# Cross-attention with residual and LayerNorm: residual sum kept in PSUM, output bias by matmul, queries projected one batch a step

## What is computed

```python
Q = (query @ Wq.T + bq).reshape(B, Sq, N_HEADS, D_K).transpose(0, 2, 1, 3)
K = (key_value @ Wk.T + bk)...
V = (key_value @ Wv.T + bv)...
scores = jnp.einsum('bhqd,bhkd->bhqk', Q, K) / np.sqrt(D_K)
attn = jax.nn.softmax(scores, axis=-1)
context = jnp.einsum('bhqk,bhkd->bhqd', attn, V)...
output = context @ W_o.T + b_o
x = output + query
mu = jnp.mean(x, axis=-1, keepdims=True)
var = jnp.mean(jnp.square(x - mu), axis=-1, keepdims=True)
return (x - mu) / jnp.sqrt(var + LN_EPS) * ln_gamma + ln_beta
```

## Time and profile before

| what | value |
|---|---|
| median of 3 runs | 232.86 us (232.59 to 237.04) |
| profiled execution, span from first to last instruction | 230.5 us |
| TensorE matmul busy | 206.8 us (90%) |
| GpSimd busy | 182.9 us (79%) |
| VectorE busy | 181.4 us (79%) |
| ScalarE busy | 172.3 us (75%) |
| mean granted TensorE clock | 0.989 of full speed |

### The profile page before, as it was taken

The page is one execution under the profiler, slowest core; times in us unless marked ns, Lnnn a source line. Parts: engine busy times, 40 slices in busy tenths (PEclk is TensorE's granted clock), DMA queues, the critical chain, the costliest instruction groups (busy, mean ns, idle before and its releaser), DMA issues.

```text
span 230.5 us, 6883 instructions
## 1 busy us (share of the span) xinstructions
PE 206.8 (90%) x2740; PEld 190.9 (83%) x2740; DVE 181.4 (79%) x378; ACT 172.3 (75%) x313; POOL 182.9 (79%) x163
## 2 busy tenths in 40 slices
PE   0999998899999899989999899989998999997930
PEld 0998797799899789978999699969996899997820
DVE  5699977378778977887888878787878787986494
ACT  4589489678778769795888588958796788887440
POOL 9999454877379958997699769975999499999873
PEclk9999999999999999999999999999999999999995
DMA  6946322345611153115321532143124111121022
GB/s 206 331 73 201 62 53 72 117 124 175 159 50 48 46 148 92 50 51 137 92 57 48 129 66 80 60 119 81 46 68 86 43 48 46 57 87 46 3 94 91
DMA packets 24808, 20.96 MB, mean 91 GB/s; under 512 B 10554, under 2 KB 21953, under 8 KB 24776
## 3 DMA queue, kind: packets, MB, share of 16 engines
q1 hardware_dynamic: 23544, 19.26, 30.1%
q10 hardware_dynamic: 1232, 1.26, 1.8%
HBM read 11.32 MB, written 4.19 MB: 67 GB/s over the span
## 4 chain that ended last, share of the span: by engine, by line
PE 52%; POOL 15%; DVE 12%; issue 10%; ACT 7%; DMA 2%; POOLq 0%; DVEq 0%; ACTq 0%
PE ps_s L348 18%; PE ps_x L348 14%; PE ps_acc L348 13%; POOL p_l L1042 9%; PE ps_d L348 6%; DVE result L905 4%; DVE xT_l L764 4%; ACT p_h L684 3%; POOL result L1050 2%; POOL x_rows L1059 2%; DMA w_raw<-in_wkT 2%; POOL rs_y L1071 2%; PE ps_x L509 1%; ACT ctx_h L691 1%; DVE vrest L796 1%
## 5 line engine op out<-in xcount | busy, mean ns | idle before, releaser
L1042 POOL TENSOR_TENSOR p_l<-p,p_h 128x512 f16<-128x512 f32 x80 | 99.1, 1243 | 34.5 <-ACT p_h L684 34.1
L850 DVE TENSOR_REDUCE maxima<-ps_d 128x4 f32<-128x308 f32 x128 | 58.8, 464 | 23.6 <-PE ps_d L348 23.2
L683 ACT ACTIVATE p<-ps_s 128x512 f32<-128x512 f32 x80 | 47.3, 592 | 21.7 <-PE ps_s L348 21.0
L348 PE MATMUL ps_acc<-vblk,p_h 128*128 128x34 bf16 (+1 forms) x960 | 52.0, 183 | 2.0 <-POOL p_l L1042 2.0
L348 PE MATMUL ps_s<-q_low,kblk 128*128 128x256 f32 x192 | 51.2, 298 | 1.1 <-issue 1.0
L348 PEld LDWEIGHTS ps_acc<-vblk,p_h 128*128 128x128 f16 x960 | 43.2, 96 | 10.3 <-issue 3.2
L348 PE MATMUL ps_acc<-vblk,p_l 128*128 128x34 bf16 (+1 forms) x640 | 48.4, 181 | 0.0
L684 ACT ACTIVATE p_h<-ps_s 128x512 f16<-128x512 f32 x80 | 47.2, 590 | 0.0
L348 PE MATMUL ps_s<-q_lo,kblk 128*128 128x256 f32 x160 | 45.0, 282 | 0.0
L348 PE MATMUL ps_d<-kblk,q_low 128*128 128x308 f32 x128 | 41.4, 327 | 0.2 <-DVE maxima L850 0.2
L348 PEld LDWEIGHTS ps_acc<-vblk,p_l 128*128 128x128 f16 x640 | 38.7, 96 | 0.0
(11 more groups left out here) (90 smaller groups left out, 446.8 us busy)
## 6 DMA issues: line engine op xcount, KB each, us to landing
xT_raw<-in_xT SPq DMA_DIRECT2D x8, 512.0 KB, 4.1
x_rows<-in_x SPq DMA_DIRECT2D x16, 256.0 KB, 2.9
out_dram<-result SPq DMA_DIRECT2D x15, 256.0 KB, 2.2
kblk<-kT SPq DMA_DIRECT2D x64, 38.5 KB, 2.3
c_raw<-in_cT ACTq DMA_DIRECT2D x4, 308.0 KB, 3.8
vblk<-vparts SPq DMA_DIRECT2D x4, 184.1 KB
rows_sb<-in_bias_rows SPq DMA_DIRECT2D x1, 384.0 KB, 7.2
kblk<-kblk SPq DMA_DIRECT2D x3, 96.0 KB, 2.4
```

The source lines that it names most:

```text
L348: return nc.tensor.matmul(o, w, m, start=start, stop=stop, skip_group_check=True)
L683: nc.scalar.activation(p32[:, n % P32SLOTS], ps_s[n % 2][:], ACT.Exp, scale=SCALE)
L850: v_.tensor_reduce(maxima[:, t, h0:h0 + DMAX_HEADS], ps_d[((DMAX + 1) * (s + 1) + j) % 2][:, 0:DMAX_HEADS * SKV] .rearrange("p (h k) -> p ...
L1042: g_.tensor_tensor(p_l[:, n % PSLOTS], p32[:, n % P32SLOTS], p_h[:, n % PSLOTS], ALU.subtract).then_inc(rest16, 1)
```

## The change

- The residual is added in place in PSUM (`residual` reads and writes the bank of `project_out`), and `statistics` and `centre` read it there; `y` in SBUF is gone. For the last batch that bank is `ps_s[0]`.
- The output bias no longer goes into `x_rows`. It is split into two rows of `bias_two`, and two matmuls of 256 columns (64 rows deep, against a selector of ones) open each `project_out`. They wait for `centred`, since they overwrite the sum of the batch before.
- Queries are projected one batch a step in steps 0 to 13 (`project_batch_q`, 12 matmuls of 256 columns, both halves in the one bank `ps_x[0]`). ScalarE writes them once (`batch_query_hi`), VectorE takes the low part (`batch_query_lo`), GpSimd copies the second form (`queries_again`).
- TensorE does the scores of two visits in a row, then the weighing of two visits; the maxima ride with the scores. The weighing of visit 2 stands ahead of `turn_maxima`.
- VectorE's list is new: the low part of the queries stands behind `centre`, and `context_lo_part` ahead of reductions 6 and 7.
- ScalarE writes the maxima after the fifth visit's exponentials; GpSimd takes the inverse roots after the third visit.

The diff, cut to what the prediction speaks of:

```diff
-        self.project_q = s % 2 == 0 and 0 <= s <= B - 4
+        self.project_q = 0 <= s <= B - 3
...
+        ps_y = [ps_s[0][:].rearrange("p a q -> p (a q)") if b == B - 1 else ps_x[1][:] for b in range(B)]
...
+            def project_batch_q(half):
+
+                cols = slice(half * SQ, (half + 1) * SQ)
+                for f in range(HALVES):
+                    ins = three(ps_x[0][:, f * SQ:(f + 1) * SQ], lambda a, k: (wq_h, wq_l)[a][:, k, f * P:(f + 1) * P],
+                                lambda b, k: (xT_h, xT_l)[b][:, k, cols])
+                ins.then_inc(pe_q, 1)
+
...
+                        pe.wait_ge(q_hi, max(HALVES, s + 2))
                         S.wait(pe, max_done, DMAX, DMAX)
                     elif j == 1:
...
-                        S.wait(pe, q_lo_done, 1, 2 - s % 2)
+                        pe.wait_ge(q_lo_done, max(HALVES, s + 1))
...
                 def project_out(*halves):
 
+                    y = ps_y[s - 1]
+                    if 0 in halves:
...
+                        if s < B:
+                            S.wait(pe, centred, QT, -QT)
+                        for qt in range(QT):
+                            mm(y[:, qt * D:(qt + 1) * D], bias_sel[:], bias_two[:], qt == 0, False)
                     S.wait(pe, ctx_lo, 1, halves[-1] if s == B else 0)
-                    if S.project_q:
-                        S.wait(pe, q_lo_done, 1, 4)
-                    else:
-                        S.wait(pe, y_done, 1, -1)
-                    if s == 1:
-                        pe.wait_ge(w_lo, 4)
...
-                            ins = chunk(ps_x[1][:, qt * D:(qt + 1) * D],
+                            ins = chunk(y[:, qt * D:(qt + 1) * D],
                                         lambda a, k: (ctx_h, ctx_l)[a][:, k, qt * P:(qt + 1) * P],
-                                        lambda b, k: (wo_h, wo_l)[b][:, k, :], k,
-                                        k == 0 and (qt == 0 or len(halves) == HALVES))
+                                        lambda b, k: (wo_h, wo_l)[b][:, k, :], k, False)
                     if HALVES - 1 in halves:
                         ins.then_inc(pe_o, 1)
 
-                def next_q(f):
+                def next_q():
...
-                    if f == 0:
+                        pe.wait_ge(k_lo, HALVES * (GROUPS - 1) + 1)
+                    if s % 2 == 0:
                         S.wait(pe, x_lo, 1, 4, by=2)
-                        S.wait(pe, ctx_lo, 1, -1)
-                    else:
-                        S.wait(pe, y_done, 1, -1)
-                    project_q(f)
-
-
-
-                tasks = {(0, 0): 0, (0, 1): 1, (1, 0): 2, (1, 1): 3, (2, 0): 4, (2, 1): 5, (3, 0): 6, (3, 1): 7,
-                         (4, 1): DMAX}
-                if S.project_q and s > 0:
-                    tasks = {(0, 0): 0, (0, 1): 1, (0, 2): 2, (1, 0): 3, (1, 2): 4, (2, 0): 5, (2, 2): 6, (3, 1): 7,
-                             (4, 1): DMAX}
-                for u in range(UNITS):
...
-                    if u == 4 and S.output and s < B:
-                        project_out(0, 1)
...
+                    S.wait(pe, ctx_lo, 1, -1)
+                    project_batch_q(s % 2)
+
+                def scores(u, *tasks):
+
+                    for n in range(2):
+                        if S.scores:
+                            score_tile(u, n)
+                        if S.maxima and n < len(tasks):
+                            max_scores(tasks[n])
+
+                def weighing(u, back):
+                    if S.output if back else S.scores:
+                        weigh(u, 0, back)
+                        weigh(u, 1, back)
+
...
+                scores(0, 0, 1)
+                scores(1)
+                weighing(3, 1)
+                weighing(4, 1)
+                if S.project_q:
+                    next_q()
+                if S.maxima:
+                    max_scores(2)
+                scores(2, 3, 4)
+                scores(3)
+                weighing(0, 0)
+                weighing(1, 0)
+                if S.output and s < B:
+                    turn_context(0, 1)
+                if S.maxima:
+                    max_scores(5)
+                scores(4, 6, 7)
+                weighing(2, 0)
+                if S.maxima:
+                    turn_maxima()
+                if S.output and s < B:
+                    project_out(0, 1)
...
+            def batch_query_hi(b):
+
+                cols = slice(b % 2 * SQ, (b % 2 + 1) * SQ)
+                for f in range(HALVES):
+                    ins = nc.scalar.activation(q_low[b // 2 % 2][:, f, cols], ps_x[0][:, f * SQ:(f + 1) * SQ], add,
+                                               bias=bq_sb[:, f:f + 1])
+                ins.then_inc(q_hi, 1)
 
...
+                    if nb >= 2:
+                        act.wait_ge(q_copied, nb - 1)
...
-                    if u == 4 and S.maxima:
-                        write_maxima()
-                    if u == 3 and S.output and s < B and S.project_q:
-                        context_hi_part(0, 1)
                     if S.scores:
                         exponentials(u)
                     if s == 0 and u < 2:
                         value_mid(V_TASKS - 2 + u)
-                    if u < HALVES and S.project_q:
-                        S.wait(act, pe_q, 1, 3 + u)
+                    if u == 1 and S.project_q:
+                        S.wait(act, pe_q, 1, 3)
                         S.wait(act, pe_s, UNITS, 0)
-                        query_hi(u, (s // 2 + 1) % 2)
-                    if u == (2 if S.project_q else 1) and S.store and s < LAST_STEP:
+                        batch_query_hi(s + 2)
+                    if u == 2 and S.store and s < LAST_STEP:
...
+                    if u == 3 and S.output and s < B:
                         context_hi_part(0, 1)
...
+            def batch_query_lo(b):
+                cols = slice(b % 2 * SQ, (b % 2 + 1) * SQ)
+                for f in range(HALVES):
+                    ins = lo_biased(q_lo[b // 2 % 2][:, f, cols], ps_x[0][:, f * SQ:(f + 1) * SQ], bq_sb[:, f:f + 1],
+                                    q_low[b // 2 % 2][:, f, cols])
+                ins.then_inc(q_lo_done, 1)
 
             def split_x():
...
                     S.wait(dve, pe_o, 1, -1)
-                    S.wait(dve, x_biased, 1, -1)
-                    if not last:
-                        S.wait(dve, centred, QT, -2 * QT)
-                    v_.tensor_tensor(y_s.rearrange("p t d -> p (t d)"), ps_x[1][:],
-                                     x_rows[:, s % 2].rearrange("p t d -> p (t d)"), ALU.add).then_inc(y_done, 1)
-
-                def statistics(t):
-                    v_.bn_stats(stats[:, t], y_s[:, t]).then_inc(stats_done, 1)
+                    S.wait(dve, ld_x[s % 2], 8, -8 * (s % 2))
+                    v_.tensor_tensor(y, y, x_rows[:, s % 2].rearrange("p t d -> p (t d)"), ALU.add).then_inc(y_done, 1)
+
+                def statistics():
+                    S.wait(dve, y_done, 1, -1)
+                    for t in range(QT):
+                        v_.bn_stats(stats[:, t], y[:, t * D:(t + 1) * D]).then_inc(stats_done, 1)
...
+                    for t in range(QT):
+                        v_.scalar_tensor_tensor(result[:, o, t], y[:, t * D:(t + 1) * D], meanvar[:, t, 0:1], gamma_sb,
+                                                ALU.subtract, ALU.mult).then_inc(centred, 1)
...
-                def queries(f):
-                    S.wait(dve, q_hi, 1, 3 + f)
-                    query_lo(f, (s // 2 + 1) % 2)
+                def queries():
+                    S.wait(dve, q_hi, 1, 3)
+                    batch_query_lo(s + 2)
...
                 when(S.output, (denominators, 0))
                 when(S.maxima, (max_of, 0))
                 when(S.output, (normalize, 0))
                 when(S.maxima, (max_of, 1))
-                when(s == B, (denominators, 1), (normalize, 1))
                 when(S.norm, (residual,))
-                when(s == B, (context_lo_part, 0))
+                when(S.output, (denominators, 1), (normalize, 1))
                 when(S.maxima, (max_of, 2))
-                if S.norm:
-                    S.wait(dve, y_done, 1, -1)
+                when(S.norm, (statistics,))
                 when(S.maxima, (max_of, 3))
-                when(S.norm, (statistics, 0))
-                when(S.project_q, (queries, 0))
-                when(s == B, (context_lo_part, 1))
-                when(S.norm, (statistics, 1))
-                when(S.output and s < B, (denominators, 1))
-                when(s == B - 1, (bias_x,))
-                if S.norm:
-                    S.wait(dve, stats_done, QT, -QT)
+                when(S.norm, (aggregate,))
                 when(S.maxima, (max_of, 4))
-                when(S.norm, (aggregate,))
-                when(S.project_q, (max_of, 5))
-                when(S.output and s < B, (normalize, 1))
-                when(S.project_q, (queries, 1))
```

(29 more changed lines are left out.)

120 lines of the change are left out of this document (57 added, 63 removed).

## The result

The changed kernel takes 254.95 us (median of 4 runs, 253.05 to 259.17) against 234.74 us for the kernel before on the same chip: **a ratio of 1.093, 95% interval 1.084 to 1.102**. Forecast were 248.7 us (239 to 258), slower with a chance of 0.84. The profiled execution has a span of 251.9 us where 246.4 was forecast. Versions are therefore compared here by their step lengths and by the time from the first scores to the end (197.3 us before, 218.7 after).

The account below looks back on a forecast made before the run. TensorE sets the pace; 11.3 us of work plus 1.9 of waits make a 13.1 us step. Steps 2 to 13 add 14.6, others 0.2, 2.0, 1.1, the rest -2: 230.5 becomes 246.4, plus 2.36 gives 248.7 us (80% range 239 to 258).

Parts of the forecast that it names:

- The first wait: TensorE's transposes of the context wait for VectorE's low part of the queries: 1.2 us in each of steps 2 to 13.
- T: Start of the transposes of the context, counted from the step's first scores: forecast at 8.42 us.
- the chain of 4.16: VectorE's unbroken work from the third maxima matmul, through reductions, statistics and centrings, to the queries' low part: 4.16 us.
- The second wait: TensorE's transposes of the maxima wait for reductions 6 and 7, behind the context's low part: 0.7 us a step.
- TM: Start of the transposes of the maxima: forecast 2.80 us behind the context's transposes, with the next step 1.89 later.
- Centring and statistics on PSUM: VectorE's forms reading PSUM, without trace rows: 0.87 us for two centrings (0.66 to 1.93), 0.74 for two statistics (0.6 to 1.0).
- The rival of a centring that stays at 1.93: Centring from PSUM no faster, 1.06 us more in VectorE's chain 12 times: 261 us, or 255 at half; chance 0.10.
- The rule weighed against the change: VectorE's fixed part is 58 cycles from SBUF, 120 from PSUM: 0.13 us more a step, 1.6 over 12 steps.
- the bias by matmul: Two 256-column matmuls on TensorE each step: 0.24 us added, bounds 0 to 0.7.
- TensorE's own work: Sum of TensorE's matmuls and transposes in a step without waits: 11.3 us, against a step of 11.89 before.
- The rival with no wait: Neither wait on the path, TensorE alone bounds at 11.3 us a step: 225.4 us, faster; chance 0.05.
- The tail: The rest behind step 14, 23.27 us before: -2 us, between 0 and -3.5.

Follow-up runs that it names:

- q_swap: Changed kernel with the queries' low part ahead of the two centrings in VectorE's list instead of behind them: 249.67 us, ratio 1.076.
- ctx_late: Changed kernel with the context's low part behind reductions 6 and 7 in VectorE's list: 251.1 us, ratio 1.070.
- no_bias: Changed kernel without the two bias matmuls a step, output bias left out of the result: 249.24 us, ratio 1.071.
- bias_128: Changed kernel with selector and bias rows 128 rows deep instead of 64, filled up with zeros: 249.38 us, ratio 1.072.
- all_three: Changed kernel with queries' low part behind reduction 3, context's low part behind reductions 6 and 7, bias matmuls ahead of the maxima's transposes: 240.4 us, ratio 1.033.
- bias_first: Changed kernel with the two bias matmuls ahead of the transposes of the maxima instead of behind them: 250.14 us, ratio 1.075.

## Why the prediction was right, and where its size was off

- **The first wait** was forecast as 1.2 us at T, 8.42 us into the step. It is 1.06 at 8.36, in 12 steps, for `q_lo`. q_swap takes two centrings out of the chain and T moves by their price; this is shown. The third maxima matmul starts 4.26 into the step, as forecast, so the chain of 4.16 is 4.10.
- **The second wait**: T to TM forecast 2.80, measured 2.81; the wait 0.54 instead of 0.7, as TensorE takes 2.27 to get there and not 2.09. ctx_late confirms that `ctx_lo` ahead of two reductions is its cause.
- **Centring and statistics on PSUM** were taken as 0.87 and 0.74 for two; they are 0.87 and 0.75. The rival of a centring that stays at 1.93 falls. Lines view of the changed kernel:

```profile
L915 DVE SCALAR_TENSOR_TENSOR result<-ps_x,meanvar,rows_sb 128x256 f32<-128x256 f32 x30 | 13.0, 476 | 0.1
L898 DVE BATCH_NORM_STATS2 stats<-ps_x 128x6 f32<-128x256 f32 x30 | 11.3, 418 | 0.0
```

- **The rule weighed against the change** (the Trainium skill, "VectorE: DVE Perf Modes", section on the TRN2 errata) would add an estimated 65 ns to each statistics instruction read from PSUM. The lines view of the kernel before has 415 ns for it, this one 418. The measurement decides: 3 ns.
- **The term that was mis-sized is the bias by matmul.** The forecast put it at 2 x 0.12 = 0.24, and TM to the next step at 1.89; it is 2.28, and the two matmuls cost 0.63 there instead of 0.24, as no_bias shows. The bound of 0 to 0.7 a step held, but the value was taken from matmuls that have neighbours of their own depth. bias_128 shows that the depth made the difference. 12 steps at 13.43 instead of 13.1 make 4.0 of the 5.5 us that the span came out above the forecast. Steps 1 and 14 add 0.39 and 0.28 by the same term: in bias_128 they take 11.97 and 10.88, and 11.9 and 10.9 were forecast. Step 0 adds 0.34 and has no bias matmul: its first weighing waits 1.99 us for GpSimd's `p_l`, where before it waited 0.76 and the forecast left this as it was.
- **TensorE's own work** was summed to 11.3 a step, and TensorE was to be busy about that long; it is busy 141.98 us in the 12 steps, 11.8 each. In all_three the shorter step is 11.90. TensorE's timeline of that run, from the transposes of the context to the next step:

```profile
114.72 0.64 PE L489 MATMUL ps_x<-ident_sb,ctx_n 128*128 128x128 f32 x4
...
116.25 0.41 PE L320 MATMUL ps_d<-kblk,q_low 128*128 128x308 f32 x1
...
117.11 0.50 PE L320 MATMUL ps_x<-bias_two,bias_sel 64*128 64x256 f32 x2
117.54 0.39 PE L424 MATMUL ps_d<-ident_sb,maxima 128*32 128x128 f32 x2
117.83 0.39 PE L320 MATMUL ps_x<-wo_h,ctx_h 128*128 128x256 f32 x1
...
119.44 0.35 PE L320 MATMUL ps_s<-q_low,kblk 128*128 128x256 f32 x1
```

  From T to the end of the weighing it takes 2.39 where the sum had 2.09, for the bias 0.43 instead of 0.24, for the output product 1.61 instead of 1.44. These make the 0.6, but not all of it is work. The last maxima matmul (116.25) starts just as the reduction that frees its bank ends; around it 0.17 more pass than in the changed kernel. The output product starts 0.29 behind the transposes and not 0.15 as in bias_first, for `ctx_lo`. And the next step starts 0.09 later than in the changed kernel, counted from the output product, when ScalarE's write has just ended (118.66 and 0.68). Without these 0.4 us the work is an estimated 11.5, worked out from these starts, and the miss is 0.2 and lies in the bias. The rival with no wait was priced too low by that, which had no weight in the result.
- **The tail** was to lose 2 us and lost 1.27. The doubt was named (a store that is issued late) but had no price of its own: the last centring waits 2.12 us for the store of the result two batches before.

```profile
247.81 0.88 DVE L915 SCALAR_TENSOR_TENSOR result<-ps_s,meanvar,rows_sb 128x256 f32<-128x256 f32 x2 [2.12 <-DMA out_dram<-result]
```

- **What stood at no cost** did so: GpSimd's copy of the queries takes 0.61 us and nobody waits for it, the weighing of visit 4 is in time. GpSimd's subtraction takes 1203 ns on average, half way between the 1.16 forecast and the 1.24 before.

Not tried: the changed kernel with the queries in a bank of their own, which would take away the reason for the first wait. The kernel's eight banks are all in use.

## What to carry to other kernels

When the pace-setting engine hands work to and fro with another, ask of each edit where the freed or added instruction stands in the other engine's list, ahead of which result: here a shorter instruction moved in front of something that is waited for cost more than a long one behind it. Summed link by link from the trace, the two waits came out within 0.2 us, but a repair wins only down to the next limit, so price that too. Try a small matmul at the depth of its neighbours, filled up with zeros, rather than as shallow as its data; here that was worth 0.38 us a step.
